# Third layer's context products spread over four stages, with a new order on VectorE and GpSimd and a second row-shift tile

## What is computed

```python
x = x + _L0_xattn_ref(_layernorm(x), ctx, mask, bias, ...)   # 32 heads of 128, attends to ctx
x = x + _L0_ffn_ref(_layernorm(x), W_base, ...)              # y = x W_base^T + b, plus 4 mixed low-rank experts
x = x + _L1_xattn_ref(_layernorm(x), ctx, Wq, bq, Wk, bk)    # one head: softmax(Q K^T / sqrt(512)) ctx
x = x + _L1_ffn_ref(_layernorm(x), qweight, ...)             # 6-bit codes: (code - zero) * scale, plus bias
```

## Time and profile before

| | us |
|---|---|
| three runs, median (lowest, highest) | 986.61 (985.14, 986.87) |
| the profiled execution | 985.75 |
| its span, first to last instruction | 983.9 |

### The profile page before, as it was taken

The page is one execution under the profiler, slowest core; times in us unless marked ns, Lnnn a source line. Parts: engine busy times, 40 slices in busy tenths (PEclk is TensorE's granted clock), DMA queues, the critical chain, the costliest instruction groups (busy, mean ns, idle before and its releaser), DMA issues.

```text
span 983.9 us, 16715 instructions
## 1 busy us (share of the span) xinstructions
PE 954.6 (97%) x5645; PEld 835.4 (85%) x5645; DVE 603.1 (61%) x1123; ACT 395.0 (40%) x1101; POOL 470.3 (48%) x528
## 2 busy tenths in 40 slices
PE   8999999999999999999999999999999997998995
PEld 7888888888898888888888888888888886776774
DVE  5674773656566566666565656565656577274874
ACT  5655443343434343433333333334343432324553
POOL 2450735464545545555555464555554511022577
PEclk9999999999999999999999999999999999899999
DMA  9233536747474656565555656464747442111001
GB/s 335 88 95 125 171 137 210 261 157 276 156 273 161 257 176 238 190 220 190 217 200 209 219 191 241 168 257 162 256 170 261 151 150 87 52 66 33 1 34 54
DMA packets 58185, 169.60 MB, mean 172 GB/s; under 512 B 5767, under 2 KB 7947, under 8 KB 57884
## 3 DMA queue, kind: packets, MB, share of 16 engines
q1 hardware_dynamic: 58140, 169.01, 48.5%
HBM read 158.51 MB, written 10.49 MB: 172 GB/s over the span
## 4 chain that ended last, share of the span: by engine, by line
PE 91%; DVE 4%; issue 2%; ACT 1%; POOL 1%; DMA 1%; SPq 0%; POOLq 0%; ACTq 0%; DVEq 0%
PE ps_q L325 6%; PE ps_q L326 6%; PE ps_q L327 6%; PE ps_v L325 6%; PE ps_v L327 6%; PE ps_v L326 6%; PE ps_o L325 6%; PE ps_o L327 6%; PE ps_o L326 6%; PE ps_t L1775 6%; PE ps_k L325 6%; PE ps_k L327 6%; PE ps_k L326 6%; PE ps_s L1748 6%; PE ps_t L1765 3%
## 5 line engine op out<-in xcount | busy, mean ns | idle before, releaser
L1203 DVE TENSOR_TENSOR acc<-ps_o,acc 128x512 f32<-128x512 f32 x128 | 87.9, 686 | 153.3 <-PE ps_o L327 153.3
L652 ACT ACTIVATE scores<-scores,neg_max 128x128 f32<-128x128 f32 x256 | 99.9, 391 | 196.3 <-DVE neg_max L1284 196.3
L325 PE MATMUL ps_v<-wv_hi,ct_hi 128*128 128x256 f32 x504 | 143.1, 284 | 1.8 <-DVE vv L1157 1.5
L327 PE MATMUL ps_v<-wv_hi,ct_lo 128*128 128x256 f32 x504 | 142.6, 283 | 0.0
L326 PE MATMUL ps_v<-wv_lo,ct_hi 128*128 128x256 f32 x504 | 142.6, 283 | 0.0
L955 POOL TENSOR_TENSOR wq_lo<-raw_q,wq_hi 128x256 fp32r<-128x256 f32 x65 | 48.2, 742 | 158.6 <-ACT wq_hi L519 158.6
L325 PE MATMUL ps_o<-wo_hi,att_hi 128*128 128x512 f32 x256 | 105.5, 412 | 0.9 <-DVE att_lo L1191 0.9
L658 ACT COPY probs_t<-ps_t 128x512 f32<-128x512 f32 x64 | 37.6, 587 | 168.1 <-PE ps_t L1765 168.1
L325 PEld LDWEIGHTS ps_v<-wv_hi,ct_hi 128*128 128x128 f32 x504 | 96.4, 191 | 6.6 <-issue 2.5
L327 PE MATMUL ps_o<-wo_hi,att_lo 128*128 128x512 f32 x256 | 100.4, 392 | 0.0
L326 PE MATMUL ps_o<-wo_lo,att_hi 128*128 128x512 f32 x256 | 100.2, 391 | 0.0
(11 more groups left out here) (335 smaller groups left out, 2396.9 us busy)
## 6 DMA issues: line engine op xcount, KB each, us to landing
ring_hi<-scratch_x_t SPq DMA_DIRECT2D x39, 512.0 KB, 4.0
ring_lo<-scratch_x_t SPq DMA_DIRECT2D x39, 512.0 KB, 5.0
ring_hi<-scratch_c_t SPq DMA_DIRECT2D x39, 512.0 KB, 4.2
ring_lo<-scratch_c_t SPq DMA_DIRECT2D x39, 512.0 KB, 5.3
raw_v<-in_w_v SPq DMA_DIRECT2D x16, 512.0 KB, 5.7
raw_o<-in_w_o SPq DMA_DIRECT2D x16, 512.0 KB, 3.3
raw_q<-in_w_q SPq DMA_DIRECT2D x15, 512.0 KB, 5.9
raw_k<-in_w_k SPq DMA_DIRECT2D x15, 512.0 KB, 5.6
```

What stands on the lines that cost most here:

```text
L325: pe.matmul(dst, hi_l, hi_r, start=first, stop=False)
L327: return pe.matmul(dst, lo_l, hi_r, start=False, stop=last)
L652: e = act.activation(probs[n][:, m, :], scores[n][:, m, :], ACT.Exp, bias=neg_max[:, n, m:m + 1], accum_out=row_sum[:, n, m:m + 1])
L1203: dve.tensor_tensor(acc[:, b, :], ps_o[:], acc[:, b, :], ALU.add).then_inc(o_added, 1)
```

## The change

Products 4 to 7 stand one to a turn in turns 0 to 3, after the closing matmul and the scores, ahead of the low-rank product. VectorE empties each in its turn and unpacks one code a turn, now ahead of `a_low`; ScalarE casts the code as the last thing of the turn. On VectorE `a_rest` stands ahead of `statistics(1, ..)`; from turn 8 on `b_finish` and the statistics for c stand ahead of `c_scale`; the shift row is made in turn 4. The row shift has two tiles in turn, the second in the place of probs_t. GpSimd does it for tiles 0 to 6 only, from turn 8 on after inv_std of c; for tile 7 VectorE does it, at the end of turn 11. The attended rows of tile 7 go to bank ps_q and wait for `a_finish` of tile 7, not for `b_finish` of tile 6.

```diff
--- before.py
+++ after.py
@@ -110,7 +110,7 @@
             scores[n], at_scores[n] = place(f"scores{n}", [P, 4, P], F32)
             probs[n] = scores[n]
             shift[n], at_shift[n] = place(f"shift{n}", [P, 4, P], F32)
-        probs_t, _ = place("probs_t", [P, 4, P], F32)
+        probs_t, at_probs_t = place("probs_t", [P, 4, P], F32)
         att_hi, at_att_hi = place("att_hi", [P, 4, P], F32R)
         att_lo, _ = place("att_lo", [P, 4, P], F32R)
         bias_sb, _ = place("bias_sb", [P, 2, 2, P], F32)
@@ -223,7 +223,7 @@
         b_probs_t, _ = place("b_probs_t", [P, P], F32, at=at_scores[0] + 512)
         z_stack, _ = place("z_stack", [P, P], F32R, at=at_scores[0] + 1024)
         b_row, _ = place("b_row", [1, D], F32, at=at_shift[0])
-        c_shift_sb, _ = place("c_shift_sb", [P, D], F32, at=at_scores[1])
+        c_shift_sb = [place(f"c_shift_sb{n}", [P, D], F32, at=(at_scores[1], at_probs_t)[n])[0] for n in range(2)]
 
 
         def bank(name):
@@ -832,8 +832,8 @@
 
                 act.wait_ge(shift_s, 1)
                 act.wait_ge(n_xn[2], b + 1)
-                wait_from(act, c_rest_s, b)
-                act.mul(c_shift_sb[:], shift_rows[:], x_sum[:, b:b + 1]).then_inc(c_shift, 1)
+                wait_from(act, c_rest_s, b - 1)
+                act.mul(c_shift_sb[b % 2][:], shift_rows[:], x_sum[:, b:b + 1]).then_inc(c_shift, 1)
 
             def stage_c(b):
                 act.wait_ge(n_t[2], b + 1)
@@ -849,13 +849,11 @@
                     stage_b(b)
                 if a < BATCH:
                     stage_a(a)
-                if w < 2:
-                    code(2 * w)
                 if 0 <= b < BATCH:
                     stage_b_exp(b)
                 if 0 <= tc < BATCH:
                     normalise_end(2, tc)
-                if 0 <= c:
+                if 0 <= c < BATCH - 1:
                     stage_c_shift(c)
                 if a < BATCH:
                     stage_a_exp(a)
@@ -865,10 +863,10 @@
                     normalise_end(0, a + 1)
                 if 0 <= b < BATCH:
                     stage_b_pt(b)
-                if w < 2:
-                    code(2 * w + 1)
                 if a < BATCH:
                     stage_a_zt(a)
+                if w < 4:
+                    code(w)
 
 
         @block.gpsimd
@@ -1095,6 +1093,13 @@
                 wait_from(pool, bs_mm, b - 1)
                 pool.tensor_scalar(r_diag[b % 2][:], ident[:], r_col[:, 1, b:b + 1], None, ALU.mult).then_inc(r_diag_s, 1)
 
+            def shift_in(c):
+                if 0 <= c < BATCH - 1:
+                    pool.wait_ge(c_shift, c + 1)
+                    pool.wait_ge(c_bias, c + 1)
+                    pool.tensor_tensor(f_scr[c % 2][:], f_scr[c % 2][:], c_shift_sb[c % 2][:],
+                                       ALU.add).then_inc(c_rest_s, 1)
+
             inv_std(0, 0)
             for w in range(BATCH + 5):
                 att, tc, c = w - 3, w - 4, w - 5
@@ -1114,12 +1119,12 @@
                     r_diagonal(w - 1)
                 if w + 1 < BATCH:
                     inv_std(0, w + 1)
-                if c >= 0:
-                    pool.wait_ge(c_shift, c + 1)
-                    pool.wait_ge(c_bias, c + 1)
-                    pool.tensor_tensor(f_scr[c % 2][:], f_scr[c % 2][:], c_shift_sb[:], ALU.add).then_inc(c_rest_s, 1)
+                if w < BATCH and 0 <= att:
+                    shift_in(c)
                 if 0 <= att < BATCH:
                     inv_std(2, att)
+                if w >= BATCH:
+                    shift_in(c)
 
 
         @block.vector
@@ -1569,7 +1574,7 @@
                 dve.reciprocal(b_sum[:, b, 1:2], b_sum[:, b, 0:1]).then_inc(b_inv, 1)
                 dve.wait_ge(b_inv, b + 1)
                 dve.wait_ge(at_mm, b + 1)
-                dve.scalar_tensor_tensor(acc[:, b, :], ps_o[:], b_sum[:, b, 1:2], acc[:, b, :], ALU.mult,
+                dve.scalar_tensor_tensor(acc[:, b, :], (ps_o, ps_q)[b // (BATCH - 1)][:], b_sum[:, b, 1:2], acc[:, b, :], ALU.mult,
                                          ALU.add).then_inc(b_add, 1)
 
             def c_rest(b):
@@ -1610,13 +1615,15 @@
                     a_finish(a - 1)
                 if has_b:
                     b_softmax(b)
+                if has_a:
+                    a_rest(a)
                 if 0 <= a - 1 < BATCH:
                     statistics(1, a - 1, a_add, a)
-                if has_a:
-                    a_rest(a)
-                if w < 2:
-                    g_evac(4 + 2 * w)
-                    unpack_code(2 * w)
+                if w < 4:
+                    g_evac(4 + w)
+                if has_att and w >= BATCH:
+                    b_finish(att)
+                    statistics(2, att, b_add, att + 1)
                 if has_c:
                     c_scale(c)
                 if has_a:
@@ -1625,20 +1632,25 @@
                     statistics(0, a + 1, o_added, ready(a + 1))
                 if has_a:
                     a_mix(a)
-                if has_att:
+                if has_att and w < BATCH:
                     b_finish(att)
                     statistics(2, att, b_add, att + 1)
-                if att == 0:
+                if w < 4:
+                    unpack_code(w)
+                if w == 4:
                     dve.wait_ge(rows_in, 48)
                     dve.scalar_tensor_tensor(shift_rows[:], zero_rows[:], -1.0, scale_rows[:], ALU.mult,
                                              ALU.mult).then_inc(shift_s, 1)
-                if w < 2:
-                    g_evac(5 + 2 * w)
-                    unpack_code(2 * w + 1)
                 if has_a:
                     a_low(a)
+                if w == BATCH + 3:
+                    last = BATCH - 1
+                    dve.wait_ge(c_bias, BATCH)
+                    dve.wait_ge(n_xn[2], BATCH)
+                    dve.scalar_tensor_tensor(f_scr[last % 2][:], shift_rows[:], x_sum[:, last:BATCH], f_scr[last % 2][:],
+                                             ALU.mult, ALU.add).then_inc(shift_s, 1)
             dve.wait_ge(c_scaled, BATCH)
-            dve.wait_ge(c_rest_s, BATCH)
+            dve.wait_ge(shift_s, 2)
             dve.wait_ge(c_add, BATCH - 1)
             dve.tensor_tensor(acc[:, BATCH - 1, :], f_scr[2 + (BATCH - 1) % 2][:], f_scr[(BATCH - 1) % 2][:],
                               ALU.add).then_inc(c_add, 1)
@@ -2147,8 +2159,12 @@
                 if b == 0:
                     pe.wait_ge(ctx_in, 32)
                     pe.wait_ge(o_added, 2 * STEPS)
-                wait_from(pe, b_add, b)
-                pe.matmul(ps_o[:], b_probs_t[:], ctx_sb[:, b, :], start=True, stop=True).then_inc(at_mm, 1)
+                if b < BATCH - 1:
+                    wait_from(pe, b_add, b)
+                else:
+                    pe.wait_ge(a_add, BATCH)
+                pe.matmul((ps_o, ps_q)[b // (BATCH - 1)][:], b_probs_t[:], ctx_sb[:, b, :], start=True,
+                          stop=True).then_inc(at_mm, 1)
 
             def c_product(b):
                 pe.wait_ge(c_lo_s, b + 1)
@@ -2172,8 +2188,8 @@
                     a_end(a - 1)
                 if has_b:
                     b_scores(b)
-                if w < 2:
-                    product_g(4 + 2 * w)
+                if w < 4:
+                    product_g(4 + w)
                 if att == BATCH - 1:
                     b_attend(att)
                 if has_c:
@@ -2188,8 +2204,6 @@
                     a_base(a)
                 if has_b and w < BATCH:
                     b_transpose(b)
-                if w < 2:
-                    product_g(5 + 2 * w)
                 if has_a:
                     a_mix_t(a)
                 if has_tc:
```

## The result

| | before | after |
|---|---|---|
| median of 20 runs each, us | 986.4 | 988.18 |
| lowest, highest | 984.95, 989.29 | 987.08, 989.23 |
| profiled execution | 985.75 | 988.05 |
| its span | 983.9 | 986.3 |

The ratio is 1.0018, 95% interval 1.0011 to 1.0025: the changed kernel is slower by about 1.8 us, which is within the 0.2% called no change. The forecast was 987.7, from a change of 1.1 us. That the time was hit doesn't say that each step was; the traces answer that.

A forecast was written before the change was run, and what follows sets the result against it. Bound by TensorE's waits in stages 0 to 4, full TensorE in 5 to 7, a GpSimd, ScalarE and VectorE chain after stage 8. Span 983.9 - 1.9 + 1.81 + 1.2 = 985.0, 1.1 more; median 987.7, range 984.6 to 989.0.

The forecast's parts named there:

- The four products: Stages 0 to 3, one product each: they cover TensorE's waits and gain 1.9 us, ends 1.4 and 2.5.
- One sign: Early stages on VectorE: if the forecast is right, no wait over 0.5 us on a_lo.
- The late statistics: VectorE's second-layer statistics come one instruction later: 0.6 us lost in stage 4, hidden in stages 5 to 7.
- the sentence on a_rest: VectorE, stages 2 to 7: a_lo ahead of the statistics takes away the 1.15 us wait, at a price of 0.6.
- at stage 8 unchanged: Stages 5 to 7: TensorE is full, the 0.6 hidden, so the whole 1.9 us gain reaches stage 8.
- GpSimd's order: After stage 8: GpSimd carries one shift more from tile 6's statistics to tile 7's bias addition, 1.42 us lost.
- The new shift's place: End of VectorE: tile 7's shift waits for GpSimd's bias addition ahead of c_lo, 5.65 against 5.26 us, 0.39 lost.
- The clock: Last product: TensorE idles some 4 us, its clock falls, six of 8 matmuls run slow: 1.2 us lost, ends 0 and 1.6.
- clock stays up: Rival for the last product: TensorE's clock does not fall, time 986.5, chance 0.15.
- faster: Rival for the end: GpSimd's chain is not last, the last c_lo does not wait, 984.2, chance 0.15.
- slower: Rival: late statistics bind in stages 5 to 7 too, 0.6 each, 1.8 in all, 989.5, chance 0.13.
- nothing: Rival: the products cover no waits of the path and the end order binds no more than before, 986.6, chance 0.12.

The follow-up runs named there:

- e6: Kernel before with only the first half of the change (products one to a turn, a_rest ahead of the second layer's statistics), old last turns: ratio 0.9979.
- e10: e6 with VectorE's statistics of the second layer ahead of a_rest again, as in the kernel before: ratio 0.9967 to before.
- e12: Changed kernel with tile 7's shift behind c_lo(7), GpSimd's old order, and second-layer statistics ahead of a_rest: 981.52 us, ratio 0.9954 to before.
- e2: Changed kernel with GpSimd's old order, its row shift ahead of the statistics step in every turn: ratio 0.9998 to before.
- e4: Changed kernel with 18 unused matmuls filling TensorE's idle time between the transposes of tile 7 and the last product: ratio 0.9996 to before.
- e1: Changed kernel with VectorE's row shift of tile 7 moved from ahead of c_lo(7) to behind it: 983.73 us, ratio 0.9965 to before.
- e7: Kernel before with only the second half of the change (new order from turn 8, VectorE's shift of tile 7), old early stages: ratio 1.0034.

## Why the forecast held

**The four products** (forecast 1.9): right. The closing matmuls of tiles 0 to 3 came at 886.04, 894.24, 904.19 and 914.49. With the 0.58 us by which this trace's small layers start sooner than before's, that is 886.62, 894.82, 904.77, 915.07, against 886.84, 895.24, 905.12 and 915.52 walked. The last is 0.45 sooner than walked, the half microsecond that was added for surpluses. The gain at the closing matmul of tile 5 is 1.88, in the part alone (e6) 1.93. One sign was not met: at 881.44 TensorE waits 0.99 us for a_lo, over the 0.5 set as the limit. That wait is of stage 0 and stood in before too, with 0.96 at 882.02, so it takes nothing from the gain; the waits for a_lo of the later tiles are gone.

**The late statistics** (0.6 in stage 4, hidden in 5 to 7): right in stage 4, 0.47 to 0.59 in size (e10, e12). From scores to scores stage 4 now takes 923.93 - 915.17 = 8.76, walked 8.77:

```profile
915.17 1.16 PE L2150 MATMUL ps_v<-gg,b_full 128*128 128x128 f32 x8 [0.18 <-ACT b_full L810]
...
923.93 0.38 PE L2150 MATMUL ps_v<-gg,b_full 128*128 128x128 f32 x1 [0.16 <-ACT b_full L810]
```

But the sentence on a_rest took it as something that pays for its price. The runs show that it does not: put back, the kernel is faster. And that the 1.9 would arrive "at stage 8 unchanged" held for the scores of tile 6 (19.77 us behind the closing matmul of tile 5, 19.79 before), not for those of tile 7: 26.33, before 26.06, with the statistics first again 26.06 (e10) and 25.98 (e12). The traces show where this comes from. In stage 7 GpSimd's row shift now starts together with VectorE's factors of the experts (alpha, 128x4), and these take 1.25 us (948.43 to 949.68) and end with GpSimd's shift (948.36 + 1.29 = 949.65); in before and e10 they begin halfway through it and take 0.64, in most other stages 0.23. VectorE's statistics behind them, and GpSimd's steps behind those, are 0.6 later.

**GpSimd's order** (1.42): 965.44 to 974.88 is 9.44 against 7.91, so 1.53; e2 gave 1.59. Another 0.28 went ahead of the statistics of tile 6 (965.44 - 933.00 = 32.44, before 967.62 - 935.46 = 32.16): the late statistics of the last paragraph, which the walk put at nothing here.

**The new shift's place** (0.39): right in mechanism, too small in size. The bias addition's start to the last addition, 5.65 by the sum without the clock, took 8.23. Of the 2.58 more, 0.96 is the instruction itself (1.65 until c_lo starts, 0.69 taken from "an equal VectorE instruction") and 1.66 the last product (978.57 to 982.38, 3.81 in place of 2.15), the rest -0.04. None of the rows of 0.69 in the earlier trace rows was equal: the remainder and the scaling read one operand from PSUM, and the last addition, which reads two from SBUF, had waited until GpSimd was through. The new shift reads two from SBUF while GpSimd works there.

**The clock** (1.2, ends 0 and 1.6): right in mechanism; the price was the upper end, 1.61 by e4, since all eight matmuls ran slow and not six. The prediction had the clock fall only once work has begun again. Here it was down some 2 us sooner: the mean granted clock (third number from the end) of TensorE's wait in after is 0.77.

```profile
973.85:978.57 4.72, 0.00 (x1) 0.01 (x1) 2.33 (x2) 0.58 (x1) 4.43 (x4) 0.77 0.15 56
```

By the Trainium skill (TensorE: Matmul & The Clock Gate, section HAM oscillation) a burst behind a wait for data may start at the slow clock; the trace agrees, here with 4.72 us of idle time and 0.43 us a matmul.

So in the traces the tail lost 4.78 where 3.0 was forecast: 0.28 + 0.11 + 0.96 + 0.46 - 0.04 = 1.77, most of it one assumed duration and one bound taken in the middle. The two parts together took 2.90 more, where the forecast had 1.1. That the median still came out at 988.18 is partly luck: the trace of before was a good run of it (985.75 against a median of 986.4 in 20 runs), and the medians differ by 1.8 where the traces differ by 2.3 in total time. The rivals: "clock stays up" is refuted by the trace of after itself (0.64 in its last window, 0.43 us a matmul), "faster" would have needed c_lo of tile 7 free of the wait, which is e1, "slower" (late statistics that bind in 5 to 7, 1.8 us) came with 0.28 of its 1.8, one stage later, and "nothing" is refuted by e6 and e7, which go to both sides.

## What to carry to other kernels

Ahead of an engine's wait, look at what is queued behind it: one instruction whose result is needed last (e1) stood ahead of the operand that the last product waited for, and cost 3.9 us; the same instruction behind that operand ran under the product. When a change nets to nothing, cut it in halves and measure them apart: here +4.5 hid -1.7, and the change with the shift moved and two orders put back gives 0.9954. Price an instruction by a row with its operands in the same memories and with the neighbour engine at the same work, not by one of equal size.
